# Node tiles 0 to 2 of the last span of a graph layer: message rows split in high and low parts, where they went whole in fp32

## The reference

```python
h_self = input @ W_self.T + b_self
H_all = einsum('rod,nd->rno', W_rel, input) + b_rel[:, None, :]   # 16 relations
agg = segment_sum(H_all[rel, tails], heads) + segment_sum(H_all[rel + R, heads], tails)
x = x + relu(h_self + agg)
# then: router logits of layernorm(x), top 2, experts: (silu(x wg) * (x wu)) wd
```

## Time and profile before

| what | value |
| --- | --- |
| median of 3 runs | 713.19 us (712.77 to 717.48) |
| profiled execution | 713.61 us |
| its span, first to last instruction | 711.5 us |
| TensorE busy | 686.6 us (97%) |
| VectorE busy | 607.0 us (85%) |
| ScalarE busy | 499.6 us (70%) |
| GpSimd busy | 299.7 us (42%) |
| mean granted TensorE clock | 0.990 |

### The profile page before, as it was taken

One profiled execution on the slowest core, in us unless ns is written; L12 is line 12 of the kernel. 1 busy time (PEld: TensorE's weight loads), 2 busy tenths in 40 slices (PEclk: granted clock), 3 DMA queues, 4 the chain that ended last, 5 costly groups with the idle time before them and its releaser, 6 DMA issues. The chain is left out here.

```text
span 711.5 us, 10496 instructions
## 1 busy us (share of the span) xinstructions
PE 686.6 (97%) x3196; PEld 543.8 (76%) x3196; DVE 607.0 (85%) x1193; ACT 499.6 (70%) x712; POOL 299.7 (42%) x255
## 2 busy tenths in 40 slices
PE   5899999999999999999998989999999999999996
PEld 4677777777777777787766867888888888888884
DVE  8669979999899777775766989999998999999982
ACT  5536458766776777876456768887787888888881
POOL 3000027785787777776870034322231233333301
PEclk9999999999999999999998999999999999999998
DMA  8347669897998989997679789999999999999952
GB/s 252 105 134 240 196 181 352 282 290 248 299 304 302 305 294 303 294 309 232 192 199 323 296 298 401 406 405 403 406 366 394 383 367 382 362 395 366 369 180 30
DMA packets 60170, 210.69 MB, mean 296 GB/s; under 512 B 9325, under 2 KB 9722, under 8 KB 47070
## 3 DMA queue, kind: packets, MB, share of 16 engines
q1 hardware_dynamic: 41534, 154.43, 57.9%
q0 software_dynamic: 18592, 55.73, 26.8%
HBM read 181.83 MB, written 28.29 MB: 295 GB/s over the span
## 5 line engine op out<-in xcount | busy, mean ns | idle before, releaser
L416 POOL DMA_INDIRECT rows_sb<-h_dram,row_of x180 | 206.8, 1149 | 156.6 <-DVE row_of L574 93.2
L584 DVE TENSOR_TENSOR rows_lo<-rows_sb,rows_hi 128x512 fp32r<-128x512 f32 x165 | 113.0, 685 | 30.3 <-ACT rows_hi L728 30.0
L871 PE MATMUL p_h<-g_hi_sb,xt_hi_whole 128*125 128x512 f32 x320 | 129.4, 404 | 0.5 <-DVE xt_lo_whole L501 0.5
L873 PE MATMUL p_h<-g_hi_sb,xt_lo_whole 128*125 128x512 f32 x320 | 127.9, 400 | 0.0
L872 PE MATMUL p_h<-g_lo_sb,xt_hi_whole 128*125 128x512 f32 x320 | 127.8, 399 | 0.0
L728 ACT CAST rows_hi<-rows_sb 128x512 fp32r<-128x512 f32 x165 | 97.5, 617 | 22.4 <-DMA rows_sb<-h_dram,row_of 16.2
L715 ACT COPY h_whole<-p_h 125x512 f32<-125x512 f32 x80 | 46.8, 586 | 85.7 <-PE p_h L873 80.2
L1250 POOL DMA_INDIRECT tokens<-token_dram,rows_of_tokens x15 | 21.8, 1456 | 171.4 <-ACT rows_of_tokens L1556 131.3
L1304 DVE TENSOR_TENSOR u_lo_sb<-stage_up,u_hi_sb 128x2048 fp32r<-128x2048 f32 x34 | 76.4, 2285 | 0.9
L1304 DVE TENSOR_TENSOR d_lo_sb<-stage_down,d_hi_sb 128x2048 fp32r<-128x2048 f32 x32 | 71.9, 2288 | 3.7 <-ACT d_hi_sb L1541 3.7
L1678 PE MATMUL p_gate<-g_hi_sb,xt_lo_whole 128*128 128x512 f32 x256 | 74.0, 400 | 0.0
(11 more groups left out here) (308 smaller groups left out, 1335.8 us busy)
## 6 DMA issues: line engine op xcount, KB each, us to landing
stage_up<-in_L_ffn_up_w SPq DMA_DIRECT2D x34, 1024.0 KB, 8.3
stage_gate<-in_L_ffn_gate_w SPq DMA_DIRECT2D x32, 1024.0 KB, 8.7
stage_down<-in_L_ffn_down_w SPq DMA_DIRECT2D x32, 1024.0 KB, 8.0
h_dram<-h_whole SPq DMA_DIRECT2D x80, 256.0 KB, 4.0
stage_up<-in_L_gnn_W_rel SPq DMA_DIRECT2D x64, 256.0 KB, 5.2
x_whole<-in_biases SPq DMA_DIRECT2D x16, 256.0 KB, 6.4
rows_sb<-h_dram,row_of POOLq DMA_INDIRECT x180, 5.3
stage_gate<-in_L_ffn_down_w SPq DMA_DIRECT2D x2, 1024.0 KB, 8.8
```

Source lines behind the costliest of these rows:

```text
L416: q.indirect_dma_start(rows_sb[:, b % ROWS], None, h_dram[0:1 + made(n) * P], bass.IndirectOffsetOnAxis(ap=row_of[:, column_of[b]:column_o ...
L584: v.tensor_tensor(rows_lo[:, b % PARTS], rows_sb[:, b % ROWS], rows_hi[:, b % PARTS].bitcast(F32), ALU.subtract).then_inc(part_lo, 1)
L871: m.matmul(o, xt_hi[:, dc, at], wt_hi_sb[:, 1 - j % 2, dc], start=(by_matmul and dc == 0), stop=False, skip_group_check=True)
L873: last = m.matmul(o, xt_lo[:, dc, at], wt_hi_sb[:, 1 - j % 2, dc], start=False, stop=False, skip_group_check=True)
```

## The change

A constant SPLIT_TILES = 3 is added. The blocks of the last span's node tiles 0, 1 and 2 (b = 165 to 173) go the split way; those of tiles 3 and 4 (b = 174 to 179) stay whole, and whole_from is 174.

- VectorE builds six last_hot in products 56 to 61 in place of fifteen. After message 164 it makes message and gate_low in turn for b = 165 to 170, then the last two gate_low, then messages 171 to 173, and only then new_tokens(0).
- ScalarE casts b = 165 to 170 in turn with the gate copies, and b = 171 to 173 after the eighth copy, ahead of root(0).
- GpSimd's gather of b waits for part_lo of b - 10 up to b = 183, so for all of them.
- TensorE uses message for tiles 0 to 2, at the same places in its order.

```diff
--- before.py
+++ after.py
@@ -49,6 +49,7 @@
 LAG, START, PACE = 4, 25, 3.0
 
 LAST_HOTS, ROUTER = 56, 72
+SPLIT_TILES = 3
 LOW, BIASES = 32, 2 * R + 1
 WEIGHTS = 2 * R + 1
 BIG = 2.0 ** 14
@@ -276,10 +277,11 @@
             span_at = {sum(T * s[3] for s in SPANS[:n]): n for n in range(len(SPANS))}
             last_span = BLOCKS - T * SPANS[-1][3]
             last_in_tile = SPANS[-1][3]
+            whole_from = last_span + SPLIT_TILES * last_in_tile
             lasts_in_told = HOT_SETS * HOT * max(IN_DIR) // TP
 
             def last_hot(b):
-                k = b - last_span
+                k = b - whole_from
                 a, k = (last_hots[0], k) if k < lasts_in_told else (last_hots[1], k - lasts_in_told)
                 return a[:, k * TP:(k + 1) * TP]
 
@@ -412,7 +414,7 @@
                         for k in range(OUTS):
                             pool.wait_ge(h_stored[k], 16 * len(range(k, made(n), OUTS)))
                     if b >= ROWS:
-                        pool.wait_ge(part_lo if b - ROWS < last_span else block_done, b - ROWS + 1)
+                        pool.wait_ge(part_lo if b - ROWS < whole_from else block_done, b - ROWS + 1)
                     q.indirect_dma_start(rows_sb[:, b % ROWS], None, h_dram[0:1 + made(n) * P],
                                          bass.IndirectOffsetOnAxis(ap=row_of[:, column_of[b]:column_of[b] + 1].bitcast(U32), axis=0)
                                          ).then_inc(gathered[b % ROWS], 16)
@@ -673,14 +675,20 @@
                         message(b)
                     if i == ROUTER + 1:
                         centre_router()
-                    if LAST_HOTS <= i < LAST_HOTS + BLOCKS - last_span:
-                        b = last_span + i - LAST_HOTS
+                    if LAST_HOTS <= i < LAST_HOTS + BLOCKS - whole_from:
+                        b = whole_from + i - LAST_HOTS
                         v.tensor_scalar(last_hot(b), seg_iota[:], seg_of[:, column_of[b]:column_of[b] + 1], None, ALU.is_equal).then_inc(last_hot_ready, 1)
                 for b in range(due(PRODUCTS), last_span):
                     message(b)
-                for k in range(2 * KC):
+                for b in range(last_span, last_span + 2 * last_in_tile):
+                    message(b)
+                    gate_low(b - last_span)
+                for k in range(2 * last_in_tile, 2 * KC):
                     gate_low(k)
                 for t in range(T):
+                    if 2 <= t + 2 < SPLIT_TILES:
+                        for k in range(last_in_tile):
+                            message(last_span + (t + 2) * last_in_tile + k)
                     new_tokens(t)
                     if t:
                         token_lows(t - 1)
@@ -803,6 +811,8 @@
                     message(b)
 
                 for k in range(2 * KC):
+                    if k < 2 * last_in_tile:
+                        message(last_span + k)
                     if k == KC:
                         act.wait_ge(self_done, 1)
                     at = slice(k % 2 * D, k % 2 * D + D)
@@ -814,6 +824,9 @@
                         x2_copy(t - 1)
                     if t == T - 1:
                         x2_copy(t)
+                    if t + 2 < SPLIT_TILES:
+                        for k in range(last_in_tile):
+                            message(last_span + (t + 2) * last_in_tile + k)
                     root(t)
                     if t < T - 1:
                         normal2(t)
@@ -909,7 +922,7 @@
 
                 def last_message(b):
 
-                    pe.wait_ge(last_hot_ready, b - last_span + 1)
+                    pe.wait_ge(last_hot_ready, b - whole_from + 1)
                     pe.wait_ge(gathered[b % ROWS], nth_round * (16 * BLOCKS // ROWS) + 16 * (b // ROWS + 1))
                     m.matmul(p_sum[0:TP, tile_of[b]], last_hot(b), rows_sb[:, b % ROWS], start=False, skip_group_check=True,
                              stop=((b - last_span + 1) % last_in_tile == 0)).then_inc(block_done, 1)
@@ -983,8 +996,11 @@
                 pe.wait_ge(round_counted, 1)
                 pe.reg_load(rounds_of(pe), n_rounds[0:1, 0:1])
                 for t in range(T):
-                    for k in range(last_in_tile):
-                        last_message(last_span + t * last_in_tile + k)
+                    for b in range(last_span + t * last_in_tile, last_span + (t + 1) * last_in_tile):
+                        if b < whole_from:
+                            message(b)
+                        else:
+                            last_message(b)
                     if t:
                         turn(t - 1)
                     if t >= 2:
```

## The result

The changed kernel takes 716.61 us (median of 20 runs, 714.95 to 721.96) against 714.71 for the kernel before (20 runs, 712.54 to 717.48). The ratio is 1.0041, with a 95% interval of 1.0029 to 1.0054: some 2.9 us slower, clear of noise and under half a per cent. (The means differ by 2.7 us; the medians by 1.9, a little less than the ratio's interval, 2.1 to 3.9 us.) The profiled execution took 717.31 us with a span of 715.5 us; 711.5 us was the span before.

The account below looks back on a forecast made before the run. TensorE, busy almost throughout, was taken to set this stretch's end by 0.68 us. A late node chain (+3.3 us), with the low clock +6.4 in all, on the 713.19 us median gave 719.6; range 715.2 to 721.7.

Parts of the forecast that it names:

- the case with the clock held: Rival: node chain starts late but TensorE's clock stays at full rate; +3.3 us, 716.5 us, chance 0.25.
- The gain on offer: TensorE, last span: nine blocks go from 0.86 to 0.46 us, 3.6 us less work where TensorE sets the end.
- VectorE's sum: VectorE before new_tokens(0): nine messages and eight gate_lows, 12.24 us, start it at 368.35 instead of 364.56, 3.8 us later.
- The second bound: Gathers alone: b=173 landing at 366.4, plus cast 0.62 and subtraction 0.60, put new_tokens(0) at 367.6.
- TensorE's gap: TensorE ahead of turn(0): idle 4.4 us, from 364.7 to 369.1, waiting for x2_ready of tile 0.
- The chain at full clock: From turn(0) through logits(0), tiles 3 and 4: new_tokens(4) at 380.7 instead of 377.36, +3.3 us.
- The clock: the step that failed: TensorE's clock falls before turn(0), returns 4.1 to 5.1 us after dense work begins at 375.0; total +6.4 us taken.
- late start, clock holds: Rival: late new_tokens(0), TensorE's clock not falling in the gap; +3.3 us, 716.5 us, chance 0.25.
- The way to the end: After tile 4, work up to the barrier is unchanged and the shift is carried whole to the kernel's end.
- The gathers: GpSimd: issue times don't move, each gather starting 0.30 us after the last, none held up by the change.
- the rival of slowed gathers: GpSimd gathers slowed beside VectorE: new_tokens(0) +2.0 more, +8.4 total, 721.6 us; chance 0.14 shared with low clock through tile 4.
- The faster rival: TensorE's 3.6 us arrive, the last gather sets the end: -2.3 us, 710.9 us, chance 0.04.

Follow-up runs that it names:

- no_late_lows: The changed kernel without the last four gate_low instructions (4 to 7), part of the computation left out; ratio to the kernel before 1.0029.
- split1_c: The changed kernel with SPLIT_TILES = 1, so only node tile 0 goes the split way; ratio to the kernel before 1.0004.
- fill_c: The changed kernel with sixteen spare matmuls on TensorE behind tile 1, in the gap ahead of turn(0); ratio to the kernel before 1.0045.
- split2_c: The changed kernel with SPLIT_TILES = 2, so node tiles 0 and 1 go the split way; median 715.57 us, ratio to the kernel before 1.0017.
- after_stats: The changed kernel with tile 2's three messages on VectorE moved behind new_tokens(0), ahead of new_tokens(1); median 716.92 us, ratio to the kernel before 1.0036.
- few_lows_c: The changed kernel without the first four gate_low instructions (0 to 3), part of the computation left out; ratio to the kernel before 1.0040.
- pe_order: The changed kernel with each turn and each token_logits one tile later in TensorE's order; ratio to the kernel before 1.0058.

## Why the prediction was right, and where it was off

The mechanism came as forecast up to new_tokens(4) at full clock. The median, 716.61 us, lies in the range of 715.2 to 721.7, but 3.0 us below the forecast of 719.6: it is inside because the range took in the case with the clock held. Of the signs named, the clock at 0.50 in 369 to 379 lasted only until between 372 and 373, and tile 3's matmuls 0.86 apart didn't come.

**The gain on offer.** TensorE did its nine blocks in less time: tile 1's last block was in at 364.33, where tile 1 ended at 366.39 before. The gain is real there and is turned into a gap.

**VectorE's sum.** Nine messages and eight gate_lows, 12.24 us, were to put new_tokens(0) at 368.35; it started at 368.09. VectorE ended message 164 at 356.01, 0.2 us later than before the change, had no wait at all after it, and needed 12.08 us. The second bound, the arrival of b=173 with its cast and subtraction, was put 0.75 us earlier. The rows have it at 366.14 + 0.62 + 0.60 = 367.36, 0.73 us earlier, and no_late_lows, where the last subtraction waits for its rows, ended on that bound.

**TensorE's gap.** 4.4 us forecast, 4.10 measured, in front of turn(0) and released by VectorE's residual sum, as said.

**The chain at full clock.** +3.3 us forecast at new_tokens(4), +3.37 measured (380.73 against 377.36). Every station fits: logits(0) at 373.3 forecast and 373.10 seen, tile 3 from 374.1 and 374.00, tile 4 from 377.9 and 377.88. The 12.64 us from new_tokens(0) to (4), through ScalarE's copy and logits(0), came again in split1_c, no_late_lows and fill_c.

**The clock: the step that failed.** It was forecast to fall ahead of turn(0); it fell just behind turn(0)'s start (1.00 up to 368.80, 0.54 in 369 to 372). The term of the sum was 3.1 us (6.4 against 3.3) and measured nothing in the profile. Two numbers in it were wrong. I had dense work begin only at tile 3, at 375.0, and set aside that the burst of tile 2 brings the clock back; the clock was back by 373, 4.2 us after turn(0) began at 368.83, ahead of everything that is on the path. And what the low clock slowed, tile 2 and turn(1), ended at 372.9, still before ScalarE's copy of tile 0 was there at 373.1: it lay beside a wait.

fill_c supports that this isn't the luck of one profile: holding the clock up gave nothing that 12 runs can tell, which leaves an average cost of up to 1.4 us open. So the case "late start, clock holds" (716.5 us, chance 0.25) gives the right size, 716.61 us, by an execution in which the clock did not hold. That the two times agree to 0.1 us is luck: it was added to 713.19 us, the median of three runs, where twenty gave 714.71, and against those the change costs 1.9 us by the medians and 2.9 by the ratio, not 3.3.

The low clock can cost time in this stretch: in split2_c tile 2 took 2.6 us longer, 2.1 of which reached new_tokens(4), in after_stats tile 3 took 2.2 us longer, and in few_lows_c, low until 374.2, new_tokens(4) came 0.16 us later, in one profile each. What makes the longest runs of the changed kernel, up to 721.96 us, stays open. fill_c, which fills the gap, has three of twelve above 720 us, so the low clock behind the gap is unlikely to be all of it.

**The way to the end.** The shift was to be carried whole to the end. At the barrier 2.96 of 3.37 us are left. TensorE's turn(4) and last logits stand at the same distance from new_tokens(4) in both profiles (1.02 and 1.48 us before, 1.03 and 1.49 after); the 0.41 us are VectorE's wait for the logits before its copy of them, which is there before the change (381.18) and not after it (384.13). Why the logits reached it later before the change isn't shown. The ratio, 2.9 us, says the same as the barrier; the medians, 1.9 us, say less.

**The gathers.** They were to keep their pace. b=173 started at 362.26 against 362.61 before, 1.34 against 1.60 from S. Beside VectorE's messages their instructions took 1.09 to 1.14 us in most cases, where 0.95 was the least: the rival of slowed gathers was right in its sign and small, as the row of 1.00 had said. The Trainium skill's rule of a port that VectorE and GpSimd lock against each other (SBUF — State Buffer, SBUF: two separate sides) isn't told apart from other causes by these runs.

The timelines of the ten profiles show more than that. In all 114 cases in which a comparison (seg_hot) starts 0.1 to 0.6 us after a gather's instruction, from 330 us on, that instruction takes 0.90 us and this distance: 1.09 us for 0.19 (366.31 and 366.50 in the changed kernel), 1.47 us for 0.57 (353.63 and 354.20 in few_lows_c). With gate_lows alone beside the instruction it took 0.95 us (363.91 before), but also 1.70 (360.98 in split1_c) and, with two gate_lows, the residual sum and the first statistics beside it, 2.30 (366.43 in after_stats), so the pace of the gathers isn't fully explained.

**The faster rival** needed new_tokens(0) before 365.3, and best shows what it takes: a start at 2.30 from S is 363.2, and then new_tokens(4) does come earlier, by 1.2 us.

## What to carry to other kernels

Work that is moved from the busiest engine to an idle one is free only up to the moment at which that engine has its next task on the chain; count the helper's whole list ahead of that task and the arrival of its last input, and take the later of the two. Removing one of two bounds that lie within a microsecond of each other shows nothing but the other. A low TensorE clock is a cost only where its slow work ends after the next wait would have ended anyway.

## What the runs showed of the hardware that I had not expected

The clock's fall and return don't follow from the gap alone. After idle times of 4.10 us (changed kernel) and 1.72 us (split2_c) before turn(0) it was low behind both. In the changed kernel it was still 1.00 up to 368.8, four microseconds into the gap, and back 4.2 us after work resumed. In few_lows_c, after the same 4.10 us, it was low from before 368 on, some two microseconds before work resumed at 369.79. In split2_c it was low from about 366 to 373, with work resumed at 366.83. In after_stats it was low for ten microseconds, though TensorE had no idle time in its rows from 371.19 on. The rows of b=173 took 3.88 us from the start of the gather's instruction to the cast that waited for them in the changed kernel (362.26 to 366.14) and 4.70 us in pe_order (362.99 to 367.69), and the gather itself started 1.34 us behind S in the one and 2.28 in the other. Together that moves this joint by as much as the edits under test.
